# Mamba block with a mixture of experts on one core: the small vectors in two groups, and the second softplus of the first chunk moved into slot 2

## The reference

```python
xn = layernorm(x)                                   # the block's input
# attn: state space model, DIN 256, 16 states, RANK 64, 4 taps
u  = rmsnorm(xn) * norm_w;  xi, z = split(u @ W_in)
xc = silu(causal_conv(xi, conv_w) + conv_b)
dt, B, C = split(xc @ W_x)                          # 64, 16, 16
dt = softplus(dt @ W_dt + b_dt)
h[t] = exp(dt * -exp(A_log)) * h[t-1] + (dt * xc) * B   # 256 x 16 states, each sequence from 0
s  = xn + (sum_states(h * C) + D_skip * xc) * silu(z) @ W_out
# ffn: top 2 of 8 experts, hidden 256, with b1, b2; relu
x  = x + s * silu(moe(xn))
```

## Time and profile before

| | us |
|---|---|
| median of 3 runs | 273.95 (273.7 to 274.05) |
| the profiled execution, its own time | 272.1 |
| its span, first to last instruction | 270.0 |
| busy: VectorE | 248.6 (92%) |
| busy: TensorE | 244.0 (90%) |
| busy: GpSimd | 238.2 (88%) |
| busy: ScalarE | 225.3 (83%) |

### The profile page before, as it was taken

The page is one execution under the profiler, slowest core; times in us unless marked ns, Lnnn a source line. Parts: engine busy times, 40 slices in busy tenths (PEclk is TensorE's granted clock), DMA queues, the critical chain, the costliest instruction groups (busy, mean ns, idle before and its releaser), DMA issues.

```text
span 270.0 us, 4176 instructions
## 1 busy us (share of the span) xinstructions
PE 244.0 (90%) x1227; PEld 130.3 (48%) x1227; DVE 248.6 (92%) x285; ACT 225.3 (83%) x432; POOL 238.2 (88%) x194
## 2 busy tenths in 40 slices
PE   6797697589999999899999899889999999999992
PEld 6443242355554723445655434436565645566441
DVE  4597899985999999899999999999999999999993
ACT  1578998899979998999899998999869885988550
POOL 7608699957999999869999999999989999898995
PEclk9999999999999999999999999999999999999998
DMA  7967990007391282025571580043698500000002
GB/s 187 296 170 156 230 237 8 6 12 163 77 207 35 50 205 61 2 74 96 124 168 30 117 195 2 0 107 68 153 209 208 138 0 0 2 0 0 2 0 78
DMA packets 18983, 26.15 MB, mean 97 GB/s; under 512 B 6684, under 2 KB 12179, under 8 KB 18963
## 3 DMA queue, kind: packets, MB, share of 16 engines
q1 hardware_dynamic: 17986, 24.71, 39.0%
q0 software_dynamic: 288, 0.53, 1.0%
q10 hardware_dynamic: 688, 0.66, 0.9%
HBM read 8.65 MB, written 1.31 MB: 37 GB/s over the span
## 4 chain that ended last, share of the span: by engine, by line
PE 37%; DVE 8%; POOL 5%; ACT 3%; issue 3%; POOLq 0%; DVEq 0%; ACTq 0%
PE px L1200 13%; PE px L1194 11%; PE py L1081 6%; DVE hs L948 5%; DVE pdbu L924 3%; POOL hc L442 3%; PE px L1173 1%; PE py L1060 1%; PE px L1143 1%; PE px L1156 1%; ACT dec L635 1%; PE px L1126 1%; PE px L1162 1%; ACT ysc L748 1%; PE px L1219 1%
## 5 line engine op out<-in xcount | busy, mean ns | idle before, releaser
L442 POOL TENSOR_TENSOR hc<-hs,Ct 128x1024 f32<-128x1024 f32 x63 | 148.9, 2377 | 4.8 <-DMA Ct<-bc_rows 2.5
L948 DVE TENSOR_TENSOR_SCAN hs<-dec,pdbu 128x1024 f32<-128x1024 f32 x62 | 138.9, 2270 | 1.1 <-POOL hc L442 1.1
L635 ACT ACTIVATE dec<-rep,negA 128x512 f32<-128x512 f32 x124 | 84.7, 723 | 0.3
L924 DVE TENSOR_TENSOR pdbu<-rep,px 128x1024 f32<-128x1024 f32 x60 | 71.1, 1218 | 2.5 <-PE px L1173 2.4
L1200 PEld LDWEIGHTS px<-w,hT 128*128 128x128 f32 x512 | 60.0, 192 | 14.5 <-ACT hT L759 6.1
L1194 PE MATMUL px<-xnT,w 128*128 128x512 f32 x128 | 64.4, 613 | 2.0 <-ACT hc L737 1.2
L1200 PE MATMUL px<-w,hT 128*128 128x128 f32 x512 | 63.5, 278 | 0.5 <-ACT hT L759 0.5
L759 ACT ACTIVATE hT<-px,cols 128x512 f32<-128x512 f32 x64 | 43.7, 689 | 8.6 <-PE px L1194 6.2
L578 POOL TENSOR_TENSOR acc<-acc,ysc 128x512 f32<-128x512 f32 x30 | 38.2, 1274 | 9.7 <-ACT ysc L748 9.3
L748 ACT ACTIVATE ysc<-px,score 128x128 f32<-128x128 f32 x120 | 33.8, 365 | 11.6 <-PE px L1200 11.5
L1081 PE MATMUL py<-hc,rsel 128*32 128x512 f32 x252 | 34.6, 604 | 2.3 <-POOL hc L442 2.3
(11 more groups left out here) (163 smaller groups left out, 265.2 us busy)
## 6 DMA issues: line engine op xcount, KB each, us to landing
rep<-dt_u SPq DMA_DIRECT2D x116, 128.0 KB, 2.4
Ct<-bc_rows SPq DMA_DIRECT2D x16, 256.0 KB, 5.3
w<-in_L_ffn_W SPq DMA_DIRECT2D x1, 1024.0 KB
x_sb<-in_L_attn_x SPq DMA_DIRECT2D x1, 768.0 KB, 5.3
out<-xn SPq DMA_DIRECT2D x3, 256.0 KB, 3.2
hc<-in_L_attn_conv_w ACTq DMA_DIRECT2D x1, 512.0 KB, 6.1
rep<-dt_u POOLq DMA_DIRECT2D x4, 128.0 KB, 3.8
win<-in_L_attn_W_in SPq DMA_DIRECT2D x1, 256.0 KB, 4.6
```

Of the source, the lines that this page charges most:

```text
L442: eng.tensor_tensor(hc[:, n % HC_RING], hs[:, n % HS_RING], Ct[:, k % 2, j:j + 1, :].to_broadcast([P, 2, CH]), ALU.mult).then_inc(hc_last ...
L635: act.activation(dec[:, n % DEC_RING, i, :], rep[:, q, 0, :], ACT.Exp, scale=negA[:, q, j:j + 1])\
L924: dve.tensor_tensor(pdbu[:, at:at + 2, :], rep[:, 2 * pair:2 * pair + 2, 1, :], B[:, None, :].to_broadcast([P, 2, CH]), ALU.mult).then_inc ...
L948: dve.tensor_tensor_scan(states.rearrange("p b t -> p (b t)"), dec[:, n % DEC_RING].rearrange("p b t -> p (b t)"), pdbu[:, at:at + 2, :].r ...
```

## The change

- The columns are made from two groups of rows in two parts of `ysc`: front (norm_w, conv_b; both loaded by SP, transposed between the two pairs of transposes of "tr") and back (b_dt, D_skip, b1; transposed behind xc0, copied by ScalarE behind the normalising of chunk 0). Eleven warming matmuls stand where there were 14.
- rsel and negA are made by GpSimd.
- e0, e1 come right behind v0 and read dt before FAR is in it. VectorE writes FAR into their PSUM banks instead (semaphore `e_far`). B0 and B1 follow, spread_u behind B0.
- v1 leaves `PRE_JOBS` for slot 2 of TensorE and ScalarE, with a softplus table load ahead of it and an exp table load after it. v0 is followed by an exp table load of its own. VectorE's times_dt(0,1) and set_far(0,1) stand in slot 5 instead of 0.

The diff, without declarations and counts:

```diff
-PRE_JOBS = ["tr", "xc0", "xc1", "dt", "tn", "v0", "v1", "B0", "e0", "e1", "B1"]
+PRE_JOBS = ["tr", "xc0", "xc1", "dt", "tn", "v0", "e0", "e1", "B0", "B1"]
-    0: ["gl", "m1b", "m0b", "z1"], 1: ["m0a", "z0"], 3: ["m1a"], 9: ["gs"], 10: ["gb"],
+    0: ["gl", "m1b", "m0b", "z1"], 1: ["m0a", "z0"], 2: ["v1"], 3: ["m1a"], 9: ["gs"], 10: ["gb"],
-    "second": [0], "gate": [1, 2, 2, 2, 3, 3, 4, 4, 4, 4, 5, 5, 8], "gate_e": [0], "gate_p": [7], "third": [9],
+    "second": [5], "gate": [1, 2, 2, 2, 3, 3, 4, 4, 4, 4, 5, 5, 8], "gate_e": [0], "gate_p": [7], "third": [9],
-BUSY = {"row": 14, "tr": 2, "xc1": 2}
+BUSY = {"row": 11, "tr": 2, "xc1": 2}
@@ SyncE
+            sp.dma_start(front[V_NW:V_NW + 1, :], norm_w.rearrange("(b p) -> b p", p=P)).then_inc(w_front, 16)
             sp.dma_start(win[:, :], W_in[:, :]).then_inc(w_in, 16)
-            sp.dma_start(rows[V_NW:V_NW + 1, :], norm_w.rearrange("(b p) -> b p", p=P)).then_inc(w_rows, 16)
-            sp.dma_start(rows[V_B1:V_B1 + 16, :], b1.rearrange("e (b p) -> (e b) p", p=P)).then_inc(w_rows, 16)
+            sp.dma_start(front[V_CB:V_CB + 2, :], conv_b.rearrange("(b p) -> b p", p=P)).then_inc(w_front, 16)
+            sp.dma_start(back[V_B1 - V_BDT:, :], b1.rearrange("e (b p) -> (e b) p", p=P)).then_inc(w_rows, 16)
@@ GpSimd
-            pool.dma_start(rows[V_CB:V_CB + 2, :], conv_b.rearrange("(b p) -> b p", p=P)).then_inc(w_rows_soft, 16)
...
+                pool.tensor_tensor(rsel[:, :], ident[:, 0:GD], ident[:, GD:2 * GD], ALU.add).then_inc(rsel_set, 1)
+                for i in range(2, GROUP):
+                    pool.wait_ge(rsel_set, i - 1)
+                    pool.tensor_tensor(rsel[:, :], rsel[:, :], ident[:, GD * i:GD * (i + 1)], ALU.add)\
+                        .then_inc(rsel_set if i < GROUP - 1 else selected, 1)
+                pool.wait_ge(expA, 1)
...
+                    pool.tensor_scalar(negA[s], alog[s, :, :, i], -1.0, None, ALU.mult).then_inc(negated, 1)
+                pool.wait_ge(vec_c, 2)
@@ ScalarE
-            act.activation(cols[:, :], pdbu[:, 2, 0:V_END], ACT.Copy).then_inc(vec_c, 1)
+            act.activation(cols[:, 0:V_BDT], pdbu[:, 2, 0:V_BDT], ACT.Copy).then_inc(vec_c, 1)
-                if job == ("v0" if k > 0 else "dt"):
+                if job == ("v0" if k > 0 else "dt") or (job, k) == ("v1", 0):
                     act.preload_act_table_set("softplus")
...
                     act.wait_ge(negated, GROUP)
+                    act.wait_ge(e_far, i + 1)
...
-                if job == "v1":
+                if job == "v1" or (job, k) == ("v0", 0):
                     act.preload_act_table_set("exp_and_others")
...
                     normalise(0)
+                    act.wait_ge(vec_t, 2)
+                    act.activation(cols[:, V_BDT:], pdbu[:, 2, V_BDT:V_END], ACT.Copy).then_inc(vec_c, 1)
+                    act.wait_ge(vec_c, 2)
@@ VectorE
-            dve.tensor_reduce(rsel[:, :], ident[:, :].rearrange("p (i d) -> p d i", i=GROUP), AX.X, ALU.add)\
-                .then_inc(selected, 1)
-            dve.wait_ge(expA, 1)
-            for i in range(GROUP):
-                s = slice(GD * i, GD * (i + 1))
-                dve.tensor_scalar(negA[s], alog[s, :, :, i], -1.0, None, ALU.mult).then_inc(negated, 1)
...
             times_dt(dve, 0, 0)
+            for i in range(2):
+                wait_filled(dve, f"e{i}", 0)
+                dve.memset(bank_of(f"e{i}", 0)[:, 0:CH:SEQ], FAR).then_inc(e_far, 1)
             set_far(dve, 0, 0)
@@ TensorE
-            pe.transpose(pdbu[:, 2, 0:V_END], rows[:, :], ident[0:V_END, 0:V_END]).then_inc(vec_t, 1)
+                if of == "front":
+                    pe.wait_ge(w_front, 16 * N_FRONT)
+                    pe.transpose(pdbu[:, 2, 0:V_BDT], front[:, :], ident[0:V_BDT, 0:V_BDT]).then_inc(vec_t, 1)
+                else:
+                    pe.wait_ge(w_rows, 16 * N_ROWS)
+                    pe.wait_ge(w_rows_soft, 16 * N_SOFT)
+                    to = GD + V_END - V_BDT
+                    pe.transpose(pdbu[:, 2, V_BDT:V_END], back[:, :], ident[GD:to, GD:to]).then_inc(vec_t, 1)
...
                             last.then_inc(tr_half, 1)
+                            columns("front")
...
                     pe.wait_ge(setup, N_SETUP + 2)
-                    pe.wait_ge(far_done, 1)
+                    wait_emptied(pe, "v0", 0)
...
-                if job == "e1":
+                if job == "xc0":
+                    columns("back")
+                if (job, k) == ("B", 0):
                     spread_u(0)
                     spread_u(1)
```

27 lines of the change are left out of this document (15 added, 12 removed).

## The result

| | before | after |
|---|---|---|
| median, us | 274.0 (272.3 to 276.2) | 276.4 (274.4 to 280.1) |
| runs | 8 | 8 |
| profiled execution, its span, us | 272.1, 270.0 | 274.4, 272.2 |

The ratio of the times is 1.007, with an interval of 1.004 to 1.011: the kernel became 1.1 to 3.0 us slower. The two profiled executions differ by 2.3 us, their spans by 2.2 us, at a mean granted clock of 0.996 and 0.997.

The account below looks back on a forecast made before the run. An opening of about 55 us sets when a VectorE-bound rest starts, through scan 2. Terms -1.1 +0.75 +1.35 +0.75 = +1.75, taken as +1.7 on 273.95: 275.65; own range 274.85 to 277.05, whole range 273.2 to 277.1.

Parts of the forecast that it names:

- scan 2: VectorE's scan of unit 2, at 37.13 before, forecast at 38.85 (+1.7); the rest follows it one for one.
- lead: Opening: small vectors in two groups bring v0 1.75 us earlier, of which 1.1 us is left from set_far on.
- wait for v1: Slot 5: VectorE reaches times_dt at 35.85, v1 is out at 36.6; a new wait of 0.75 us.
- port: Slot 5: times_dt, with two SBUF inputs, waits for GpSimd's product of unit 1 to end; +1.35 us.
- moved times_dt, MEMSET: VectorE's times_dt(0,1) and its MEMSET, moved from the opening to ahead of scan 2; +0.75 us.
- share that is left at set_far: Opening: set_far(0,0) now waits behind matmuls, 1.55 to 1.65 us after v0's end; of 1.75 us only 1.1 is left.
- rival without a port conflict: times_dt runs beside GpSimd in 0.67 us, scan 2 at +0.5, ScalarE's path decides at +0.8: 274.75; chance 15%.
- Table drain: Rival: each of v1's two added table loads costs 2.66 us, shift +3.6, 277.55; chance 5%.
- Behind the scan: SP's 16 issues take 9.6 to 11 us, Bt lands 3.6 us later; 0.1 to 1.4 us on top, nothing taken.
- ScalarE's path: v1's move makes ScalarE reach the silu table load about 0.8 us late (50.2 instead of 49.4), second to VectorE's path.

Follow-up runs that it names:

- e1: Kernel after, but times_dt(0,1) takes one factor from PSUM instead of SBUF: 274.89 us, ratio 1.003 to the kernel before.
- e11: Kernel after plus four matmuls that add zero where TensorE idles: 274.97 us, ratio 1.006 to the kernel before.
- e12: Kernel before plus four matmuls that add zero where TensorE idles: 272.76 us, ratio 0.997 to the kernel before.
- e4: First half of the change alone, v1 left ahead of the loop without added table loads: 273.1 us, ratio 0.995 to the kernel before.
- e9: e6 with Bt's load sent ahead of the 16 replica DMAs: 276.22 us, ratio 1.009 to the kernel before.
- e8: e4 with C sent ahead of pair 1's replicas: 276.85 us, ratio 1.012 to the kernel before.
- e2: Kernel after, but v1 uses Relu without its two table loads: 277.32 us, ratio 1.009 to the kernel before.
- e6: Kernel after, but GpSimd does times_dt(0,1) and set_far(0,1): 276.3 us, ratio 1.007 to the kernel before.
- e7: e4 with W_in loaded first again: 272.96 us, ratio 0.997 to the kernel before.

## Why the prediction was right, step by step

The forecast of 275.65 on 273.95, +1.7 us, met +2.0 by the ratio (+2.4 by the medians), and scan 2 moved by +2.22 where +1.7 was forecast. Its four terms:

| term, us | forecast | in the trace |
|---|---|---|
| lead, at the end of unit 3's product | −1.1 | −0.66 |
| wait for v1 | +0.75 | +0.95 |
| port | +1.35 | +1.11 |
| moved times_dt, MEMSET | +0.75 | +0.82 |
| scan 2 | +1.7 | +2.22 |

The third column: the product ended at 36.27 (33.27 + 3.00), 0.66 ahead of the 36.93 of before; L451 started 0.95 later; it took 1.80 where 0.69 is its time without the conflict (e1); the 0.69 itself and the rest up to 39.35, less the 0.20 that lay between product and scan before, are 0.82. The wait and the port come out again in e11 (1.00 us, and 1.74 less 0.69). The lead does not stand so firmly: it is the difference of two single openings, and openings of one kind lie up to 2 us apart (e12), so that the sum came so near is in part luck.

**The lead was mis-sized.** It is the term that failed: v0 came 0.95 us earlier instead of 1.75. About half of what is missing is lost ahead of the columns, which were out by 7.92 and not by 7.45. It was not conv_b that held them up in this trace but the warming matmuls. TensorE's timeline of the kernel after, then of the kernel before:

```profile
2.03 5.06 PE L1061 MATMUL pdbu<-ident 128*128 128x128 f32 x22 [2.03 <-POOL ident L465]
6.88 0.63 PE L1135 MATMUL px<-ident,xr 128*128 128x128 f32 x2
7.45 0.26 PE L1069 MATMUL pdbu<-ident,ysc 3*128 3x3 f32 x1
```

```profile
2.03 4.93 PE L1048 MATMUL pdbu<-ident 128*128 128x128 f32 x28 [2.03 <-POOL ident L463]
```

The eleven (22 instructions) took 5.06 us, no less than the fourteen before, where the working had scaled the 4.93 down to an end near 5.9. TensorE worked off 6 or 7 instructions in each microsecond from 5 to 7, and 9 before; why is not shown, the granted clock is 1.00 in the rows of both. The first pair of transposes so began at 6.88 instead of 6.1, and front's at 7.45 instead of 7.0. In other traces it was conv_b after all: in e4, e9 and e11 front waited 0.84 to 1.33 us for it, to between 7.83 and 8.44. The xrT copy started 1.38 us earlier than before, and the other half was lost behind it, where front was taken as the only thing to wait for. But the first tap product began at 8.33 (7.39 in the kernel before), because W_in landed 6.7 us after its issue and not 4.6, and the four took 1.73 us (1.29 before). TensorE's second convolution waited 0.36 us for them, from 10.20 to 13.87, and the second xc, dt and v0 hang on its end. The working took this chain as unchanged, although the change puts a DMA ahead of W_in on SP's queue; it looked at what stands behind win, and not at win itself. That the order of loads is the cause is not shown: one order gave starts 1.2 us apart. The profile's row of the DMA issues, in the kernel after:

```profile
win<-in_L_attn_W_in SPq DMA_DIRECT2D x1, 256.0 KB, 6.7
```

**The share that is left at set_far was right.** Of v0's lead the forecast took 0.65 us away, since set_far now stands behind e1's matmuls; the trace has 0.59 us of idle there, set_far 1.50 us behind v0's end (forecast 1.55 to 1.65, before 0.96). Then the 4th replica DMA, landing 4.9 us after its issue (5.1 in the earlier trace rows), lets the first decay go, with ScalarE idle 0.93 us ahead of it. e8 shows from the other side that this landing carries the opening. The end of unit 3's product, though, is set by GpSimd's first product and so by C: its last issue ended 0.45 us earlier than before (26.99 against 27.44) and it landed 0.66 earlier, which is the −0.66 of the table.

**The wait for v1** stood as foretold on ScalarE's order decay, table, v1: 36.51 + 0.69 = 37.20 against 36.6, all of the 0.6 us being the lost lead.

**The port** was right as a mechanism and near in size. By e1 it is worth 1.22 us at scan 2, and 1.2 in the time with overlapping intervals. The rival without a port conflict (274.75), for which 0.67 us beside L534 spoke, is ruled out by that: a small operation of GpSimd does not hold a VectorE instruction as a 128 x 1024 product does. What the prediction did not say is that wait and port are not independent. e2 shows it: without the wait the port only takes longer. In the sum the two stand as separate terms, which works only because they were laid end to end on one time axis.

**Table drain** is ruled out. v1 started 0.02 us behind the end of its table load (35.21 + 1.28 = 36.49), the next decay 0.01 us behind the second; with the load gone v1 came 1.40 us earlier, a load and a little. The figure of the Trainium skill, "ScalarE: Activation LUTs", section "What ACT_TABLE_LOAD costs", about 1.38 us more for each switch, would make that 2.66 us: the runs disagree with it.

**Behind the scan.** SP's 16 issues took 10.05 us from 39.18, and Bt went out at 49.27, inside the forecast. It landed 2.1 us later, where 3.6 was taken, at 51.4, and GpSimd reached it at 52.48: 0.1 to 1.4 us were worked out and 0 taken. The 0 was right, with 1.1 us to spare, because the landing was shorter than the 3.6 us that the working had used (with those, Bt would have been there at 52.9). e6 shows how close the next bound is: with the 16 issues 1.1 us later it costs 1.93 us of waiting. SP's timeline of the kernel after:

```profile
39.18 10.05 SPq L340 DMA_DIRECT2D rep<-dt_u  x16
49.27 0.59 SPq L401 DMA_DIRECT2D Bt<-bc_rows  x1
```

ScalarE's path was forecast at +0.8; its silu table load is at 51.64 and not at 49.4, +2.2. It is later than its own path made it, since by then it follows VectorE's, but in e6, with VectorE's delay gone (scan 2 at 36.85) and the clock at 1.00 up to 50, it is at 50.82: the "ScalarE is second" of the prediction holds, and its +0.8 is too small, +1.4 in this trace.

**What the sum left out is the clock.** It was 1.00 in both profiled runs in this stretch, so the rows of before didn't show it, and the forecast of spans did not need it (+2.2 in spans, +2.2 with both kernels filled). But the median of either kernel has some of it in it, 0.9 us by e12 and 0.5 to 1.4 by e11, depending on whether ratios or medians are compared. It may be why e7's gain of 1.6 us in the trace was gone in the time, and e2 is slower than after at the same scan 2 (its clock was 0.977 in the profiled run). The clock isn't all of the scatter either: over 86 runs of before the correlation of the mean clock with the time is only −0.3.

## What to carry to other kernels

A VectorE instruction with two SBUF inputs that is moved beside a long GpSimd product costs up to that product's length: keep it where GpSimd has no long product, or give it an operand from PSUM, and lay its wait and the port on one time axis, since removing the wait alone only made the instruction stand longer. An engine that starts earlier gains nothing if the next one on the chain starts later: e4's scan came 1.8 us earlier, and its split of B did not. A number of warming matmuls is not a time: eleven took 4.3 to 5.1 us here. When a step is moved later, look for all that stands behind its DMAs in the same queue (here B's load behind 16 copies), and when a load is moved earlier, for the one it overtakes. And take a second trace of the same program before reading tenths out of one: two of the program before (itself and e12) had scan 2 at 37.13 and 39.28. Ahead of a stretch in which TensorE is on the critical path, fill its gaps: a few matmuls that add zero into an open accumulation were worth 0.9 us in before and 1.5 to 1.7 in e7, as much as any reordering tried here, and somewhere between 0.5 and 1.4 in after, where the intervals do not separate it from nothing.
